# Expert layer of a decoder kernel: 128-row slots with plain fp32 products, and rows added to their tokens in memory

## What is computed

```python
# x2 = x1 + cross_attention(...);  n = layernorm(x2)
prob = softmax(n @ classifier_w.T)            # 12 choices, 8 real experts and 4 that return n itself
top2 = indices of the 2 largest of prob + bias
out = x2
for c in top2:
    w = 1.5 * prob[c]
    out += w * (down[c] @ (silu(gate[c] @ n) * (up[c] @ n)))   # c < 8, inner width 256
    out += w * n                                               # c >= 8
```

## Time and profile before

| | us |
|---|---|
| median of 3 runs (lowest, highest) | 2459.24 (2457.08, 2464.03) |
| the profiled execution | 2460.55 |
| its span, first to last instruction | 2458.8 |
| PE busy in the span | 2173.5 (88%) |
| DVE, ACT, POOL busy | 1405.2, 977.7, 896.4 |
| mean granted TensorE clock, as a share of 2.4 GHz | 0.944 |

### The profile page before, as it was taken

How to read it: one execution, slowest core, us unless ns; L and a number is a source line. 1 busy time by engine, 2 the same in 40 slices (tenths; PEclk the granted TensorE clock), 3 DMA queues, 4 the chain that set the end, 5 groups by cost and what they waited for, 6 DMA issues and landing times. The chain is left out here.

```text
span 2458.8 us, 35777 instructions
## 1 busy us (share of the span) xinstructions
PE 2173.5 (88%) x10448; PEld 1660.2 (68%) x10448; DVE 1405.2 (57%) x3086; ACT 977.7 (40%) x1960; POOL 896.4 (36%) x906
## 2 busy tenths in 40 slices
PE   5689999995799997799999999999998799749991
PEld 3678888883677775566666666666665578637771
DVE  3635555554888886365555555555555255535554
ACT  2313333334233322355555555555555222125660
POOL 2400000001666666334232232332334355346664
PEclk8899999997899998899999999999999899869996
DMA  8621212125345454242222222222211344264336
GB/s 288 171 73 38 65 34 67 34 79 174 111 135 152 137 153 156 75 124 59 79 59 64 61 58 66 58 60 80 59 51 34 108 105 105 51 208 129 104 105 196
DMA packets 293922, 244.00 MB, mean 99 GB/s; under 512 B 151906, under 2 KB 258898, under 8 KB 290386
## 3 DMA queue, kind: packets, MB, share of 16 engines
q1 hardware_dynamic: 273186, 190.42, 26.6%
q10 hardware_dynamic: 14160, 34.22, 3.8%
q0 software_dynamic: 6496, 18.37, 2.7%
HBM read 149.42 MB, written 93.53 MB: 99 GB/s over the span
## 5 line engine op out<-in xcount | busy, mean ns | idle before, releaser
L2239 DVE TENSOR_REDUCE ca_top<-ca_ps_s 112x1 f32<-112x487 f32 x256 | 168.8, 659 | 241.3 <-PE ca_ps_s L2051 241.3
L2140 ACT ACTIVATE ca_prob<-ca_ps_s,ca_down,ca_scales 112x487 f32<-112x487 f32 x256 | 194.0, 758 | 194.1 <-DVE ca_down L2243 194.1
L1975 POOL TENSOR_TENSOR ca_k<-ca_k 125x512 f32<-125x512 f32 x64 | 81.1, 1268 | 484.6 <-DVE ca_k L2224 484.6
L2051 PE MATMUL ca_ps_s<-ca_kT,ca_qT 128*112 128x487 f32 x512 | 231.9, 575 | 0.8 <-issue 0.8
L75 PE MATMUL out_ps_y<-out_w_hi,out_o_hi 128*128 128x512 f32 x448 | 187.6, 419 | 42.4 <-DVE out_o_lo L1208 16.5
L2067 PE MATMUL ca_ps_o<-ca_pT,ca_v 125*128 125x448 f32 (+1 forms) x512 | 204.9, 542 | 0.6 <-ACT ca_pT L2148 0.6
L75 PE MATMUL ca_ps_p<-ca_w_hi,ca_c_hi 128*125 128x512 f32 x384 | 174.5, 454 | 24.9 <-POOL ca_c_lo L1969 24.9
L77 PE MATMUL out_ps_y<-out_w_hi,out_o_lo 128*128 128x512 f32 x448 | 180.5, 403 | 0.0
L76 PE MATMUL out_ps_y<-out_w_lo,out_o_hi 128*128 128x512 f32 x448 | 180.4, 403 | 0.0
L599 POOL COPY sa_val<-lat_v 112x128 f32<-112x128 f32 (+1 forms) x64 | 18.9, 296 | 409.7 <-PE sa_ps_o L656 409.4
L2067 PEld LDWEIGHTS ca_ps_o<-ca_pT,ca_v 125*128 125x128 f32 (+1 forms) x512 | 97.7, 191 | 102.4 <-issue 101.6
(11 more groups left out here) (291 smaller groups left out, 5694.0 us busy)
## 6 DMA issues: line engine op xcount, KB each, us to landing
self_outT<-sa_ov SPq DMA_DIRECT2D x64, 224.0 KB, 2.4
out_o_raw<-self_outT SPq DMA_DIRECT2D x56, 256.0 KB, 2.9
cross_qT<-out_qt SPq DMA_DIRECT2D x56, 256.0 KB, 2.6
ca_qT<-cross_qT SPq DMA_DIRECT2D x64, 224.0 KB, 2.8
cross_outT<-ca_ov SPq DMA_DIRECT2D x64, 224.0 KB, 3.1
out_o_raw<-cross_outT SPq DMA_DIRECT2D x56, 256.0 KB, 3.8
ffn_raw<-in_expert_w SPq DMA_DIRECT2D x8, 1536.0 KB
ca_c_first<-in_ctxT SPq DMA_DIRECT2D x15, 750.0 KB, 5.1
```

The costliest lines, as they stand in the source:

```text
L1975: pool.tensor_tensor(k1[0:m, :], k1[0:m, :], k2[0:m, :], ALU.add).then_inc(k_added.sem, 1)
L2051: pe.matmul(ps_s[j % 2][:, :], qT[i % 2][:, j, :], kT[par][:, i, :], start=True, stop=True).then_inc(scored.sem, 1)
L2140: act.activation(prob[j][:, 0:KV], ps_s[j % 2][:, :], ACT.Exp, bias=down[:, j:j + 1], scale=scales[par][:, n:n + 1], accum_out=total[:, j: ...
L2239: dve.tensor_reduce(top[:, j:j + 1], ps_s[j % 2][:, :], AX.X, ALU.max, negate=True).then_inc(topped.sem, 1)
```

## The change

In `experts`: a slot has 128 rows (`ST = P`), and the formula for `NS` gives 35 slots, one unit each. Products are plain fp32 with the weights read where they lie in `raw`, at an address that PE takes from a register; the splits and low parts go. A list entry has two words, the token and its weight as a float. ACT scales by the weight as it evicts the output. POOL adds the 128 rows to rows of a tensor `x3` in memory (in the code `rows_y`), which SP has filled from `acc` ahead of it, by an indirect transfer with `compute_op=ALU.add`; each of these waits until the one before has landed. At the end SP copies `x3` to the output in one transfer. Filler entries name 128 spare rows behind the 1792. In `cross_output`, `locate` makes the two-word entries, and DVE and POOL build the filler.

```diff
-ST = 2 * P
+ST = P
...
@@ cross_output, locate
-                dve.tensor_scalar(id_i[par][:, :], ids_f[:, bass.ds(t, 1)], 0.0, None, ALU.add)
+                dve.tensor_scalar(entry[par][:, :, 0], ids_f[:, bass.ds(t, 1)].broadcast_to((P, 2)), 0.0, None, ALU.add)
+                dve.tensor_tensor(portions[:, :, :], oh[:, t, :].rearrange('p (c e) -> p c e', c=2), over_heads(weight[:, t, :], 2), ALU.mult)
                 then(1, dve.tensor_tensor(spot[:, 0:E], place[:, t, :], base[:, 0:E], ALU.add))
+                dve.tensor_reduce(entry[par][:, :, 1].bitcast(F32), portions[:, :, :], AX.X, ALU.add)
...
@@ experts
-    NU = 2 * NS
-    AHEAD = 2
+    NU = NS
+    AHEAD = 4
+    LEAD = 5
...
             sp.dma_start(raw[:, 0, :], weights[0]).then_inc(w_in, 16)
+            sp.dma_start(rows_y[0:T, :].rearrange("(t p) d -> p t d", p=P), acc[:, :, :]).then_inc(acc_put, 16)
+            sp.dma_start(rows_y[T:T + P, :], acc[:, 0, :]).then_inc(acc_put, 16)
...
-            for t in range(TT):
-                sp.wait_ge(summed, 2 * t + 2)
-                sp.dma_start(out[t * P:(t + 1) * P, :], acc[:, t, :]).then_inc(stored, 16)
+            sp.wait_ge(put.sem, put.at(NU - 1))
+            sp.dma_start(whole(out), whole(rows_y[0:T, :])).then_inc(stored, 16)
...
+            def add(h, i):
+                s = h * 4 + i
+                pool.tensor_copy(spot_i[i % 2][:, :], list_i[:, bass.ds(s, 1), 0]).then_inc(spotted.sem, 1)
+                wait(pool, spotted, s)
...
+                wait(pool, y_out, s)
...
+                if not isinstance(s, int) or s:
+                    wait(pool, put, s, -1)
+                    pool.sem_inc(y_free.sem, 1)
+                pool.indirect_dma_start(rows_y, bass.IndirectOffsetOnAxis(ap=spot_i[i % 2][:, 0:1], axis=0),
+                                        yt[i % 4][:, :], None, compute_op=ALU.add).then_inc(put.sem, 16)
...
+            for s in range(LEAD):
                 prepare(0, s)
+            pool.wait_ge(acc_put, 32)
+            for i in range(4):
+                prepare(0, i + LEAD)
+                add(0, i)
...
+            def expert(h, i):
+                e = pe.value_load(who_i[0:1, bass.ds(h * 4 + i, 1)], min_val=0, max_val=E - 1)
+                pe.wait_ge(w_in, e * 16 + 16)
+                pe.sem_inc(ticks, 1)
+                return raw[:, bass.ds(e, 1), :].rearrange("p o w -> p (o w)")
...
                 for k in range(KD):
-                    mm = mm3(pe, ps_g[i % 2][:, :], xh[i % 2][:, k, :], xl[i % 2][:, k, :], gu_of(w_hi[b])[:, k, :],
-                             gu_of(w_lo[b])[:, k, :], k == 0, k == KD - 1)
+                    mm = pe.matmul(ps_g[i % 2][:, :], xT[i % 2][:, k, :], w[:, k * 2 * INTER:(k + 1) * 2 * INTER],
+                                   start=(k == 0), stop=(k == KD - 1))
...
             def copy_y(h, i):
                 n = h * 4 + i
+                act.activation(portion[i % 2][:, :], list_i[:, bass.ds(n, 1), 1].bitcast(F32), ACT.Copy).then_inc(portioned.sem, 1)
                 wait(act, down_mm, n)
...
+                wait(act, y_free, n, -4)
+                act.activation(yt[i % 4][:, :], ps_y[i % 2][:, :], ACT.Copy, scale=portion[i % 2][:, 0:1]).then_inc(y_out.sem, 1)
```

More of the change, by code:

```diff
@@ L1467, in cross_output @@
         ids_f = sb('ids_f', [P, TT])
-        id_i = [sb(f'id_i{i}', [P, 1], I32) for i in range(2)]
-        fill = sb('fill', [P, (DUMP + P) // P], I32)
+        entry = [sb(f'entry{i}', [P, 2, 2], I32) for i in range(2)]
+        portions = sb('portions', [P, 2, TOTAL])
+        fill = sb('fill', [P, (DUMP + P) // P, 2], I32)
+        fill_i = sb('fill_i', [P, (DUMP + P) // P], I32)
         ps_c = ctx.bank('ps_c', P, 2, E)
@@ L2324, in experts @@
         list_i = sb("list_i", [P, NS, 2], I32)
-        row_i = [sb(f"row_i{i}", [P, 2], U32) for i in range(2)]
-        fetch = sb("fetch", [P, TT, 2, E])
-        fetch_f = sb("fetch_f", [P, TT, 2])
-        fetch_i = sb("fetch_i", [P, TT, 2], U32)
-        share = sb("share", [P, TT, 2])
+        row_i = [sb(f"row_i{i}", [P, 1], U32) for i in range(4)]
+        spot_i = [sb(f"spot_i{i}", [P, 1], U32) for i in range(2)]
+        portion = [sb(f"portion{i}", [P, 1]) for i in range(2)]
         ps_x = [ctx.bank(f"ps_x{i}", P, KD, P) for i in range(2)]
@@ L2337, in experts @@
         w_in = ctx.sem("weights_loaded")
-        list_in = ev("lists_loaded", 1, step=16)
-        ticks = ctx.sem("ticks")
+        list_in = [ev(f"lists_loaded{i}", 1, step=16) for i in range(4)]
+        ticks, act_ticks = ctx.sem("ticks"), ctx.sem("act_ticks")
         row_ready = ev("row_indices", 1)
@@ L2350, in experts @@
         turned = ev("a_turned", 1, 2)
-        a_hi, a_lo = ev("aT_hi", 1), ev("aT_lo", 1, 2)
+        a_kept = ev("aT_kept", 1, 2)
         down_mm = ev("down", 1, 4)
         y_out = ev("y_copied", 1, 2)
-        y_put = [ev(f"y_stored{i}", 1, 1, 16) for i in range(2)]
-        fetched = [ctx.sem(f"y_fetched{i}") for i in range(4)]
-        summed = ctx.sem("summed")
+        acc_put = ctx.sem("acc_stored")
+        portioned = ev("portion_ready", 1)
+        spotted = ev("row_spots", 1)
+        put = ev("rows_added", 1, 0, 16)
+        y_free = ev("y_free", 1, 4)
         stored = ctx.sem("stored")
@@ L2403, in prepare @@
                 wait(pool, row_ready, s)
                 carry(pool, h, ticks)
-                for half in range(2):
-                    pool.indirect_dma_start(xg[2 * b + half][:, :], None, rows_n,
-                                            bass.IndirectOffsetOnAxis(ap=row_i[b][:, half:half + 1], axis=0))\
-                        .then_inc(x_in[2 * b + half].sem, 16)
-                wait(pool, g_hi, s)
-                carry(pool, h, ticks)
-                pool.tensor_tensor(w_lo[b][:, 0:GW], raw[:, bass.ds(e, 1), 0:GW].rearrange("p o w -> p (o w)"),
-                                   w_hi[b][:, 0:GW], ALU.subtract).then_inc(g_lo.sem, 1)
@@ new lines, in _ @@
+            for s in range(LEAD):
+                prepare(0, s)
+            pool.wait_ge(acc_put, 32)
+            for i in range(4):
+                prepare(0, i + LEAD)
+                add(0, i)
+            with pool.Fori(1, (NS - LEAD) // 4) as h:
+                for i in range(4):
+                    prepare(h, i + LEAD)
+                    add(h, i)
+            for s in range((NS - LEAD) // 4 * 4, NS):
+                if s + LEAD < NS:
+                    prepare(0, s + LEAD)
+                add(0, s)
@@ L2437, in _ @@
             down_mm.open(pe)
+            pe.wait_ge(planned, 1)
             def turn_x(h, i):
                 n = h * 4 + i
-                pe.wait_ge(x_in[i % 4].sem, (h + i // 4) * 16 + 16)
-                if not (isinstance(h, int) and i < 2):
-                    wait(pe, x_lo, n, -2)
+                wait(pe, x_in[i % 4], h + i // 4)
+                wait(pe, x_kept, n, -2)
                 for k in range(KD):
@@ L2493, in _ @@
             y_out.open(act)
-            for i in range(2):
-                y_put[i].open(act)
-            def split(h, i, part):
-                s, b = h * 2 + i, i % 2
-                e = act.value_load(who_i[0:1, bass.ds(s, 1)], min_val=0, max_val=E - 1)
-                act.wait_ge(w_in, e * 16 + 16)
-                wait(act, (gu, down_mm)[part], h * 4 + 2 * i, -3)
-                act.sem_inc(ticks, 1)
-                cols = (slice(0, GW), slice(GW, WW))[part]
-                act.activation(w_hi[b][:, cols], raw[:, bass.ds(e, 1), cols].rearrange("p o w -> p (o w)"), ACT.Copy)\
-                    .then_inc((g_hi, d_hi)[part].sem, 1)
+            x_kept.open(act)
+            a_kept.open(act)
+            y_free.open(act)
             def turn_x(h, i):
@@ L2512, in turn_x @@
                 wait(act, gu, n, -2)
-                act.activation(xh[i % 2][:, :, :], ps_x[i % 2][:, :, :], ACT.Copy).then_inc(x_hi.sem, 1)
+                act.activation(xT[i % 2][:, :, :], ps_x[i % 2][:, :, :], ACT.Copy).then_inc(x_kept.sem, 1)
             def sigmoids(h, i):
```

166 lines of the change are left out of this document (51 added, 115 removed).

## The result

The changed kernel takes 2419.89 us (median of 4 runs, 2414.90 to 2422.45), the kernel before, measured beside it, 2458.48 (4 runs, 2457.08 to 2464.03): a ratio of 0.983, 95% interval 0.981 to 0.986. The forecast was 2440 us in a range of 2416 to 2490. The sign is as forecast and the time lies in the range, but the gain is 38.6 us where 19 were forecast, so terms of the sum are off by as much as the forecast itself.

What follows compares the result with a forecast made beforehand. PE's pace bounds the units; a store-and-gather end follows. First turn 2181.7, units 231 (202.0 + 14 + 15) and end 26.7 give a span of 2439.4, forecast as 2440 us, range 2416 to 2490.

Steps and rivals of the forecast that it cites:

- The register loads on PE: Two loads per unit in PE's stream, taken as partly hidden: 0.4 us per unit, 14 us; 54 us if wholly bare.
- the stage before: Stage ahead of the experts: two small DVE instructions per tile, larger filler and more columns cost about 1.2 us.
- the store of `acc`: Start of the experts' stage: 3.67 MB queued behind the first expert's weights delays the second expert's weights by 14 us.
- what bounds the units: Units of the experts' stage: PE sets the pace, 4.79 us per unit before the change, with no gap.
- the price of a unit of plain products: Units on PE: 5.15 us of products plus 0.62 of turns, 5.77 us; 35 units make 202.0 us.
- ACT's weight copies: Beside PE's products in the units: removing them gains nothing, since their price on the path is zero.
- the losses in the first 60 us: Start of the units: slow clock, a wait and first adds beside loads lose 15 us, where it was 25; 8 to 28 possible.
- The wait of some 5 us: Early units: one wait of PE, with the slow clock behind it, stays the same; part of the 15 us start loss.
- The adding transfers: Output adds per unit: each lands in 5.7 us, just under PE's 6.17 us, so taken as hidden behind PE.
- Rival A: Units: the chain of adding transfers becomes the bound, from a step of 6.0 us; each further microsecond costs 35; chance 0.24.
- The end: After PE's last product: eviction, last add, issue, copy and close take 26.7 us, replacing 51.8 us of store, gathers and additions.
- rival C: End of the kernel: the last copy takes twice the time, 30 us, giving 2453 us; chance 0.12.

## Why the prediction was right and wrong

Two steps made the gain come out twice as large as forecast. The register loads on PE were put at 14 us and cost none in the steady state, and the stage before was put at +1.2 us where it became some 9 us shorter (11.3 by the profiles). A third, the store of `acc` ahead of the gathers, was put at nothing before the first turn and cost 8.7 us, which hid most of the second.

**Right: what bounds the units.** PE's pace does, and the price of a unit of plain products (5.77 forecast, 5.81 measured) held, as did 35 x 5.77 = 202.0 (203.4). That ACT's weight copies cost nothing in the steady state held too: the run with plain fp32 alone still has them, at the same 5.81. For the subtractions there is only the row of before without a gap; in the first 60 us they may be part of the 15.9 us of losses that went in that run.

**Wrong in size: the register loads.** The forecast took "a quarter to a third of the bound, 0.4 us per unit: 14 us". It is 0 in the steady state, shown by the runs without and with twice the loads at the same pitch, and four times the loads show where the cover ends. The evidence that PE runs ahead was in the text, but I then counted only the turns ahead of the load as cover. The gaps of some 0.65 us put down to "issue" in the first 60 us, about twice as long with the loads doubled and absent without them, fit a load on an empty array.

**Wrong in size: the losses in the first 60 us.** Forecast 15 us (8 to 28); from the first turn to the last product's end, 2391.98, it is 214.05 - 203.4 = 10.7. The run with plain products alone already had 9. The wait of some 5 us, which I carried over as "the same", was in fact two waits for gathers of 4.3 and 4.2 us; behind the start of the units the longest is now 1.39. The adds beside the weight loads, which stood in this term, are in the chain above.

**Wrong: the start, both ways.** Two terms hid each other, and that the first turn is off by no more than 3.8 us is luck. The store of `acc` I put behind the first expert's weights as a delay of the second expert only. It delayed lists and gathers, 8.7 us, which the run with the store held back shows. The experts' stage, where I had +1.2 us, began 11.3 us earlier, of which the layout of the list explains 9 to 10 by the medians. In the sum the first turn came 3.8 us earlier than forecast. The stage before was priced by instructions added, and the transfer they feed was not looked at: POOL's 26.5 us of waiting for its own scatters stood in the trace of before, and a change of the layout on which it acts was in the diff. The row that I took for a scatter, 2.9 us from issue to landing, was the last one; the median of the 28 is 5.4.

**The adding transfers.** Forecast 5.7 us and hidden. They land in 4.8, but POOL's issue takes 1.60 in place of 0.96, and the step is 5.5 to 5.7 us. Hidden beside 5.81, by 0.1 to 0.3 us. The margin forecast, 6.17 - 5.9, was made of a loads term that does not exist and a landing that was too long. Rival A came only for the first adds, but it was nearer than the sum suggests: by an estimate from this margin, another microsecond per step would have shown with 0.7 to 0.9 us in each of 35 units.

**The end.** Forecast 26.7, measured 2420.2 - 2391.98 = 28.2. The copy with what lies around it takes 14.5 us where SP's issue, copy and close were put at 20.4, and rival C is out. Against that, the chain of adds lags PE when PE stops: from the last product's end to the copy's issue it is 13.75 us where eviction and one add gave 6.3. The two errors, -5.9 and +7.4, nearly cancel, so that the end came out within 1.5 us is luck too. (Rival C's saving at the end was also miscounted: with its copy the end would be 39.4 us and the saving 12, not 10.)

Together, against the forecast span of 2439.4: first turn -3.8, pace +1.4, loads -14, losses -4.3, end +1.5, in all -19.2, which is 2420.2.

## What to carry to other kernels

When a change touches the layout that a transfer writes, look in the trace at who waits for that transfer, even if the edit counts only two small instructions; here it was worth some 9 us of time, where the whole rearrangement of the products gave 12.6. Ask of each transfer put ahead in a queue what small transfers land behind it, and expect that a delayed burst moves a part of its cost instead of removing it; here half. A serial chain that is hidden by a few tenths of a microsecond appears where its transfers land late and where its cover ends, so its lag belongs in the sum of the start and of the end.

## What was new about the hardware

- An indirect transfer of 128 words of 4 bytes lands in 4.9 to 5.4 us at the median when places of one list are neighbours, in 3.5 at 8 bytes apart, 2.2 at 32. With entries of 8 bytes it is 3.3 to 3.8 side by side and 2.1 at 32.
- An indirect transfer with an add of 256 KB occupies POOL for 1.60 us and lands in 4.8 at the median (the first, beside weight loads, in 9.1); the same without add 1.01 and 2.8.
- A register load on PE takes 0.30 us. Two per group of products leave no gap in the steady state, four leave 1.1 to 1.7 us ahead of the projection.
- A copy of 3.67 MB from memory to memory lands in 14.0 us, at the measured time 262 GB/s of data.
